# A chunked state-space scan inside a fused network: the order of SyncE's loads, and the place and buffers of the column sums of squares

## The chip, the cores and the metric

The kernel runs on one core of a Trainium2 chip. The metric is the device time of one execution in microseconds, lower is better.

## What is computed

The kernel computes a whole block of layers on a float32 input x of 2 x 1024 x 128: a small feed-forward layer, attention, the feed-forward layer again, a mixture of experts with 8 experts, a bidirectional Mamba-2 layer, and the mixture of experts again. The change touches the Mamba-2 layer only. For each direction it is, cut to what matters:

```python
z, xBC, dt = split(u @ Wi.T)
xBC = silu(conv4(xBC) + conv_b)
x, Bm, Cm = split(xBC)
dt = softplus(dt + dt_bias); A = -exp(A_log)
h = h * exp(dt_t * A) + (dt_t * x_t) B_t        # for each time step t, from h = 0
y = einsum(h, C_t) + D * x
y = y * silu(z)
y = y * rsqrt(mean(y * y) + 1e-5) * norm_w      # mean over the 256 channels
out = y @ Wo.T
x = x + 0.5 * (out_forward + out_backward)
```

## The kernel before, in words

The layer has four units: two batches times two directions (`UNITS`). A unit has 8 chunks of 128 time steps, so there are N = 32 chunks, g = 8u + i, where i is called the step below. The recurrence is done in chunks. Within a chunk a 128 x 128 matrix of decays per head takes the place of the time loop, and a state h is passed from chunk to chunk. All five engines run a program written out by hand, each a loop over g in its own order, and they meet only at semaphores; an engine that waits holds up all that is behind it in its program.

What happens for chunk g, with the lines of the profile:

- SyncE, `spread_rows` (L1917): one DMA spreads the four rows of running sums of the chunk over all 128 partitions into `cums[g % 2]` (L1922). It waits until ScalarE's Relus have read the place (`lowered`). If i > 0, two more DMAs bring the exponentials of these sums, the decays, into `e_cum[g % 2]` (L1929). They wait for `y_read` of g - 1, which is VectorE's read of the outputs of chunk g - 2. Ahead of chunk 16, `keep_rows` writes the sums of the second batch to DRAM and waits for the write.
- TensorE, `before` (L2053): transposes of x, the product of B and C, and a transpose of B (L2067) that raises `b_done`.
- ScalarE, `exps` (L2072): four Relus on `cums` (L2081), a copy of the transposed B to `mb_bs` (L2086, waits for `b_done`), one exponential (L2088).
- VectorE, `front`: `xdt` (L2106), `gm` (L2110), `mt` (L2113, waits for the exponential).
- GpSimd, `to_state` (L2125) and `decay` (L2144); TensorE, `state` (L2136); VectorE, `pass_state` (L2159).
- TensorE, `outputs` (L2168, L2172, L2178), all into one PSUM bank; VectorE, `back` (L2191, L2193), which raises `y_read`.
- The gate, y * silu(z) (L2202), on GpSimd in units 0 to 2 and on VectorE in unit 3; ScalarE squares the result into `y2[g % 2]` (L2211); GpSimd adds the two halves, `pair` (L2215); TensorE multiplies with a column of ones, `squares` (L2228), which gives the sum of squares of 128 time steps.
- Once per unit: `variance` on VectorE (L2235) and `deviation` on ScalarE (L2242, a square root, which needs its own activation table, as the exponential and the silu do).
- The output projection of unit u - 1 runs within unit u, in three parts: TensorE `output` (L2258), VectorE `add` (L2269 to L2276), at steps 3, 4 and 5. It shares a PSUM bank with the column sums, so `squares` waits for `out_read` of the parts that were added before.

Beside this, unit u prepares unit u + 1: TensorE projects (L2005) in pieces, ScalarE takes them (L2019) and makes the first tap of the convolution (L2032), VectorE makes the other three (L2041), two of them at each of the steps 0 to 5, and at step 6 ScalarE runs four silus over 1024 columns (L2048) and those of z. In unit 3 GpSimd scatters the rows of one routing for the next mixture of experts (L1555) between its other work, and the last scatter has to be done before the second mixture can load its first slots.

In loop g the engines work in this order. TensorE: `before(g+1)`, `state(g)`, projections, `outputs(g)`, `squares(g-2)`, `output`. ScalarE: `exps(g+1)`, `square(g-1)`, then `deviation`, takes and taps. VectorE: `front(g+1)`, `pass_state(g)`, `back(g)`, `add`, taps. GpSimd: `to_state(g+1)`, gate of g, `decay(g+1)`, `pair(g-1)`.

## Time and profile before

| | |
|---|---|
| runs | 864.51, 865.79, 862.6 us; median 864.51 |
| the profiled execution | 858.66 us, its span 856.9 us |
| TensorE matmuls busy | 717.7 us (84%) |
| ScalarE busy | 544.5 us (64%) |
| VectorE busy | 494.1 us (58%) |
| GpSimd busy | 300.5 us (35%) |
| stretch of the scan | about 491 to 695 us |

The busy shares are averages over stages that differ: in the attention stage ScalarE and TensorE are full, in the mixtures TensorE is, in the scan it is VectorE for most of the time. A share over the span says little about what a change in one stage is worth. The profiled execution lies below the three timed runs, so terms that are read from it are applied as a difference.

### The profile page before, as it was taken

Reading aid. Unit: us, or ns where it says so; the run is one execution under the profiler, and the core shown is the slowest. Engines: PE = TensorE matmul, PEld = TensorE weight load, DVE = VectorE, ACT = ScalarE, POOL = GpSimd, SP = SyncE. Lnnn points to the kernel's source line nnn. Section 1 sums busy time; section 2 is a strip of 40 time slices with the busy share of each in tenths; the row PEclk is TensorE's granted clock in tenths of the full one; section 3 lists DMA queues with packets and bytes.
Section 4 is the critical chain, followed back from the end, with each engine's and each line's share of the span. In section 5 each row is a group of like instructions: output and inputs, shape, how many; then the busy total and the mean of one; then the engine's idle time right before and its main releaser. Section 6 shows DMA issues by size and latency. Waiting matters only on the chain.

```text
span 856.9 us, 12889 instructions
## 1 busy us (share of the span) xinstructions
PE 717.7 (84%) x3968; PEld 372.2 (43%) x3968; DVE 494.1 (58%) x1450; ACT 544.5 (64%) x938; POOL 300.5 (35%) x331
## 2 busy tenths in 40 slices
PE   4799999989999879877889886888878868899981
PEld 1432222212232225544556454666556645556650
DVE  6876532215754747632656479787898857233341
ACT  5378997989989976523456775966967514234440
POOL 3090003301000515264123555444642832644343
PEclk9899999999999999997989988889998978899996
DMA  4057652521791202111211031212221311111313
GB/s 129 2 197 181 149 112 54 214 83 50 263 211 51 87 25 60 30 53 38 72 28 55 26 108 46 69 43 66 73 69 40 109 48 31 58 47 51 86 44 94
DMA packets 76361, 69.70 MB, mean 81 GB/s; under 512 B 9732, under 2 KB 60281, under 8 KB 76032
## 3 DMA queue, kind: packets, MB, share of 16 engines
q1 hardware_dynamic: 70880, 60.04, 25.0%
q0 software_dynamic: 5120, 8.68, 3.1%
q8 instruction: 35, 0.57, 0.3%
q14 instruction: 38, 0.31, 0.1%
q10 hardware_dynamic: 288, 0.10, 0.1%
HBM read 40.70 MB, written 29.18 MB: 82 GB/s over the span
## 4 chain that ended last, share of the span: by engine, by line
PE 27%; DVE 12%; issue 10%; ACT 7%; POOL 3%; DMA 2%; SPq 0%; POOLq 0%; DVEq 0%; ACTq 0%
PE ps_main L1628 11%; PE ps_main L1658 8%; DVE mb_act L2041 4%; PE ps_side L2005 1%; PE ps_main L1589 1%; PE ps_main L1624 1%; POOL moe_slots L1555 1%; ACT mb_act L2048 1%; DMA moe_back<-moe_rows 1%; PE ps_main L1699 1%; ACT mb_e_seg L2081 1%; DVE moe_hid L1653 1%; POOL moe_rows L1726 1%; DVE mb_h L2159 1%; DVE mb_xdt L2106 1%
## 5 line engine op out<-in xcount | busy, mean ns | idle before, releaser
L685 ACT ACTIVATE attn_p<-attn_ps 128x1024 f32<-128x1024 f32 x256 | 240.5, 1059 | 34.2 <-PE attn_ps L701 19.9
L1628 PE MATMUL ps_main<-moe_xsT,moe_w 128*128 128x320 f32 x384 | 131.8, 471 | 18.7 <-issue 9.9
L701 PE MATMUL attn_ps<-attn_p,attn_v 128*32 128x512 f32 x1024 | 136.6, 604 | 3.9 <-issue 3.7
L1638 ACT ACTIVATE moe_act_h<-ps_main 128x320 f32<-128x320 f32 (+1 forms) x128 | 55.2, 433 | 115.9 <-PE ps_main L1628 53.1
L1653 DVE TENSOR_TENSOR moe_hid<-moe_act_h,ps_main 128x320 f32<-128x320 f32 (+1 forms) x128 | 62.0, 485 | 113.3 <-ACT moe_act_h L1638 48.8
L1555 POOL DMA_INDIRECT moe_slots<-rows,moe_scatter_at x64 | 63.5, 991 | 98.1 <-issue 34.5
L678 PE MATMUL attn_ps<-attn_q_rows,attn_k_rows 64*128 64x512 bf16 x448 | 84.0, 385 | 12.2 <-ACT attn_p L685 5.3
L1628 PEld LDWEIGHTS ps_main<-moe_xsT,moe_w 128*128 128x128 f32 x384 | 70.3, 200 | 53.8 <-issue 34.4
L1658 PE MATMUL ps_main<-moe_hid,moe_w 128*128 128x320 f32 (+1 forms) x256 | 80.9, 493 | 7.9 <-issue 4.7
L678 PEld LDWEIGHTS attn_ps<-attn_q_rows,attn_k_rows 64*128 64x128 bf16 x448 | 20.4, 92 | 134.3 <-ACT attn_p L685 119.3
L1726 POOL DMA_INDIRECT moe_rows<-moe_y,moe_dest x48 | 46.1, 961 | 87.0 <-ACT moe_y L1719 63.3
L2041 DVE SCALAR_TENSOR_TENSOR mb_act<-mb_padded,mb_taps,mb_act 128x1024 f32<-128x1024 f32 x48 | 67.1, 1408 | 3.1 <-ACT mb_act L2032 2.6
L1658 PEld LDWEIGHTS ps_main<-moe_hid,moe_w 128*128 128x128 f32 (+1 forms) x256 | 45.1, 208 | 40.0 <-issue 22.7
L2081 ACT ACTIVATE mb_e_seg<-mb_cums,mb_cum_col 128x128 f32<-128x128 f32 x128 | 40.7, 389 | 28.6 <-DMA mb_cums<-mb_cum_kept 28.6
L1193 POOL TENSOR_TENSOR x_sb<-x_sb,bout_half 128x1024 f32<-128x1024 f32 (+1 forms) x4 | 7.3, 1830 | 103.7 <-DVE rows L1148 103.7
L2202 POOL TENSOR_TENSOR mb_z<-mb_y_in,mb_z 128x256 f32<-128x256 f32 x24 | 26.2, 1093 | 49.2 <-DVE mb_y_in L2193 37.1
L434 POOL TENSOR_SCALAR attn_parts<-attn_q 128x512 bf16<-128x512 f32 x4 | 2.5, 617 | 111.8 <-DVE attn_q L396 111.8
L701 PEld LDWEIGHTS attn_ps<-attn_p,attn_v 128*32 128x32 f32 x1024 | 20.5, 107 | 41.4 <-issue 36.2
L2113 DVE TENSOR_TENSOR mb_mt<-mb_e_seg,mb_gm 128x512 f32<-128x512 f32 x32 | 26.7, 836 | 17.6 <-ACT mb_e_seg L2088 9.9
L1726 POOL DMA_INDIRECT moe_rows<-mb_y,moe_dest x24 | 22.9, 955 | 34.9 <-ACT mb_y L1719 28.8
L2005 PE MATMUL ps_side<-norm_xT,mb_w_xbc 128*128 128x512 f32 x64 | 31.7, 616 | 3.2 <-DVE mb_ab L1974 1.9
L2136 PE MATMUL ps_main<-mb_xw,mb_bs 128*128 128x256 f32 x56 | 19.8, 438 | 15.5 <-DVE mb_h L2159 10.7
(268 smaller groups left out, 1283.5 us busy)
## 6 DMA issues: line engine op xcount, KB each, us to landing
mb_cums<-mb_cum_kept SPq DMA_DIRECT2D x32, 256.0 KB
moe_slots<-zeros SPq DMA_DIRECT2D x4, 1380.0 KB, 13.7
attn_q_rows<-attn_q_parts SPq DMA_DIRECT2D x36, 128.0 KB
attn_k_rows<-attn_k_parts SPq DMA_DIRECT2D x36, 128.0 KB
moe_w<-in_w SPq DMA_DIRECT2D x3, 1536.0 KB, 11.7
moe_rows<-zeros SPq DMA_DIRECT2D x4, 1024.0 KB, 15.1
moe_back<-moe_rows SPq DMA_DIRECT2D x16, 256.0 KB, 3.3
mb_e_cum<-mb_e_cum_kept SPq DMA_DIRECT2D x56, 64.0 KB
```

The lines of the kernel that those rows point to most:

```text
L678: ins = self.core.nc.tensor.matmul(into, self.k_rows[rows, ring, pair, keys], self.q_rows[rows, ring, pair, queries], start=True, stop=True)
L685: self.core.nc.scalar.activation(self.p[:, w % self.PB, :, :].rearrange("p a n -> p (a n)"), self.ps_s[:, w % self.SB, :, :].rearrange("p ...
L701: ins = self.core.nc.tensor.matmul(self.ps_av[32 * i:32 * i + 32, :], self.v[:, b * TPB + kt, HGROUPS * i + m, :], self.p[:, w % self.PB, ...
L1555: nc.gpsimd.indirect_dma_start(self.slots[r], bass.IndirectOffsetOnAxis(self.scatter_at[:, b, k, j:j + 1], 0), self.row_of[:, b * TPB + j, ...
L1628: self.core.nc.tensor.matmul(ps[:, w % 2, 0:CAP], wt[:, e, c * P:(c + 1) * P], self.xsT[:, u % 2, :], start=True, stop=True).then_inc(self ...
L1638: self.core.nc.scalar.activation(self.act_h[into, w % 2, :], self.ps_h1[rows, w % 2, 0:CAP], ACT.Silu).then_inc(self.silu_done, 1)
L1653: self.core.nc.vector.tensor_tensor(self.hid[rows, u % 2, c, :], self.act_h[rows, w % 2, :], bank[rows, w % 2, 0:CAP], ALU.mult)\
L1658: return self.core.nc.tensor.matmul(self.y_bank(u)[:, 0:CAP], self.w2[rows, u % E_, c, :], self.hid[rows, u % 2, c, :], start=start, stop= ...
L1726: self.core.nc.gpsimd.indirect_dma_start(self.rows[u // E_], bass.IndirectOffsetOnAxis(self.dest[0:n, u % self.OUT, s:s + 1], 0), self.y[u ...
L2005: self.core.nc.tensor.matmul(bank[:], weight, self.xT[:, t0:t0 + BANK], start=True, stop=True).then_inc(self.proj_done, 1)
L2041: ins = self.core.nc.vector.scalar_tensor_tensor(out, src, tap, out, ALU.mult, ALU.add)
L2081: ins = nc.scalar.activation(self.e_seg[:, g % 2, hh, :], self.cums[:, g % 2, hh, :], ACT.Relu, bias=self.cum[:, di, n, hh:hh + 1], scale= ...
```

## The change

Three things are changed, all in the scan.

1. SyncE's loads. `spread_rows` is split into `spread_sums` and `spread_decays`. Chunks 0 and 1 are as before. From there the order is sums(2), sums(3), decays(2), sums(4), decays(3), and so on: the sums of chunk g come ahead of the decays of chunk g - 1. The conditions that each waits for are unchanged.
2. The column sums of squares. `y2` has three places in place of two (1 KB more in each partition), ScalarE's `square` waits accordingly for the column sum of three chunks earlier, and TensorE runs `squares(g-3)` ahead of `outputs(g)` where it ran `squares(g-2)` behind it. In the last three loops it is as before (loop 29 has both).
3. The scale of a finished unit. VectorE's `variance` of unit u - 1 moves within step 2 from ahead of `front` to behind `back`; ScalarE's `deviation` moves from step 2 to step 3.

```diff
-        self.y_in, self.y_old, self.y2 = sb("y_in", [P, 2, 2, P]), sb("y_old", [P, 2, 2, P]), sb("y2", [P, 2, 2, P])
+        self.y_in, self.y_old, self.y2 = sb("y_in", [P, 2, 2, P]), sb("y_old", [P, 2, 2, P]), sb("y2", [P, 3, 2, P])
...
-    def spread_rows(self, sp, g):
+    def spread_sums(self, sp, g):
         u, di, b, i, n, cols = self.at(g)
         j = n % TPB
         if g >= 2:
             sp.wait_ge(self.lowered, g - 1)
         sp.dma_start(self.cums[:, g % 2, :, :], self.cum_dram[b, di, j].unsqueeze(0).to_broadcast([P, NH, P])).then_inc(self.cums_in[g % 2], 16)
+
+    def spread_decays(self, sp, g):
+        u, di, b, i, n, cols = self.at(g)
+        j = n % TPB
         if i == 0:
             return
         if g >= 2:
...
-        if g >= 2:
-            act.wait_ge(self.ss_done, g - 1)
-        self.core.nc.scalar.activation(self.y2[:, g % 2, :, :], self.z[:, u % 2, :, cols], ACT.Square).then_inc(self.squared, 1)
+        if g >= 3:
+            act.wait_ge(self.ss_done, g - 2)
+        self.core.nc.scalar.activation(self.y2[:, g % 3, :, :], self.z[:, u % 2, :, cols], ACT.Square).then_inc(self.squared, 1)
...
+                    parts = (0 if u == 0 else PARTS_OUT * (u - 1) + min(max(i - 3, 0), PARTS_OUT)) + (u == 3 and i == 7)
+                    if 3 <= g < N - 2:
+                        mamba.squares(pe, g - 3, parts)
                     mamba.outputs(pe, g)
-                    if g >= 2:
-                        mamba.squares(pe, g - 2, (0 if u == 0 else PARTS_OUT * (u - 1) + min(max(i - 3, 0), PARTS_OUT)) + (u == 3 and i == 7))
+                    if g >= N - 3:
+                        mamba.squares(pe, g - 2, parts)
...
                         for g in range(2):
-                            mamba.spread_rows(sp, g)
+                            mamba.spread_sums(sp, g)
+                            mamba.spread_decays(sp, g)
                         moe.fetch(sp, 1)
-                        for g in range(2, N):
+                        for g in range(2, N + 1):
                             if g == 2 * NC:
                                 mamba.keep_rows(sp, 1)
-                            mamba.spread_rows(sp, g)
+                            if g < N:
+                                mamba.spread_sums(sp, g)
+                            if g >= 3:
+                                mamba.spread_decays(sp, g - 1)
...
-                    if u >= 1 and i == 2:
-                        mamba.variance(dve, u - 1)
                     if u == 3 and i == 6:
                         mamba.variance(dve, 3)
...
                     mamba.back(dve, g)
+                    if u >= 1 and i == 2:
+                        mamba.variance(dve, u - 1)
...
-                    if u >= 1 and i == 2:
+                    if u >= 1 and i == 3:
                         mamba.deviation(act, u - 1)
```

## Rows read from the trace of the kernel before

**Rows 1.** Busy time over four stretches of the scan: this is their sum.

```profile
sum 204.00, PE 163.04 PEld 118.71 DVE 167.05 ACT 145.05 POOL 110.65; mean PE 40.76 PEld 29.68 DVE 41.76 ACT 36.26 POOL 27.66
```

**Rows 2.** Waits of ScalarE, 491 to 695 us: total, times, longest.

```profile
ACT mb_e_seg L2081 <- DMA mb_cums<-mb_cum_kept: 28.6, 15, 3.6
```

**Rows 3.** Waits of SyncE's queue, 491 to 695 us.

```profile
SPq L1929 <- DVE mb_y_in L2193: 119.9, 21, 12.9
```

**Rows 4.** Timeline of SyncE: start, duration, instruction.

```profile
622.79 1.24 SPq L1929 DMA_DIRECT2D mb_e_cum<-mb_e_cum_kept  x2
...
629.73 1.23 SPq L1929 DMA_DIRECT2D mb_e_cum<-mb_e_cum_kept  x2
631.00 0.59 SPq L1922 DMA_DIRECT2D mb_cums<-mb_cum_kept  x1
```

**Rows 5.** Timeline of ScalarE in unit 2; in brackets the idle time before.

```profile
613.65 1.28 ACT L2242 ACT_TABLE_LOAD   x1
...
634.51 1.28 ACT L2081 ACTIVATE mb_e_seg<-mb_cums,mb_cum_col 128x128 f32<-128x128 f32 x4 [3.56 <-DMA mb_cums<-mb_cum_kept]
```

**Rows 6.** Timeline of VectorE, units 1 to 3.

```profile
564.59 0.42 DVE L2191 TENSOR_TENSOR mb_y_old<-mb_e_cum,ps_main 128x256 f32<-128x256 f32 x1 [1.77 <-PE ps_main L2178]
...
576.64 0.87 DVE L2276 SCALAR_TENSOR_TENSOR x_sb<-ps_main,mb_rstd,x_sb 128x128 f32<-128x128 f32 x3
...
589.48 2.89 DVE L2041 SCALAR_TENSOR_TENSOR mb_act<-mb_padded,mb_taps,mb_act 128x1024 f32<-128x1024 f32 x2
...
600.86 0.69 DVE L2113 TENSOR_TENSOR mb_mt<-mb_e_seg,mb_gm 128x512 f32<-128x512 f32 x1 [3.12 <-ACT mb_e_seg L2088]
...
620.69 0.96 DVE L2113 TENSOR_TENSOR mb_mt<-mb_e_seg,mb_gm 128x512 f32<-128x512 f32 x1 [0.52 <-ACT mb_e_seg L2088]
...
646.00 0.18 DVE L1142 RECIPROCAL norm_rstd<-norm_std 128x4 f32<-128x4 f32 x1 [1.86 <-ACT norm_std L1113]
```

**Rows 7.** Timeline of GpSimd in unit 3.

```profile
664.36 0.61 POOL L2125 TENSOR_TENSOR mb_xw<-mb_xdt,mb_to_end 128x256 f32<-128x256 f32 x1 [2.04 <-DVE mb_xdt L2106]
...
692.53 0.99 POOL L1555 DMA_INDIRECT moe_slots<-rows,moe_scatter_at  x1 [0.16 <-issue]
```

**Rows 8.** Timeline of ScalarE at the turn from unit 1 to 2.

```profile
583.54 0.42 ACT L2211 ACTIVATE mb_y<-mb_z 128x256 f32<-128x256 f32 x1 [0.96 <-POOL mb_z L2202]
587.31 1.28 ACT L2081 ACTIVATE mb_e_seg<-mb_cums,mb_cum_col 128x128 f32<-128x128 f32 x4 [3.35 <-DMA mb_cums<-mb_cum_kept]
588.57 0.27 ACT L2086 COPY mb_bs<-ps_main 128x128 f32<-128x128 f32 x1
...
591.65 4.26 ACT L2048 ACTIVATE mb_act<-mb_act,mb_conv_b 128x1024 f32<-128x1024 f32 x4
...
596.67 0.60 ACT L2019 ACTIVATE mb_z<-ps_side 128x512 f32<-128x512 f32 x1 [0.28 <-PE ps_side L2005]
```

**Rows 9.** Timeline of TensorE's matmuls in unit 1.

```profile
576.56 1.06 PE L2168 MATMUL ps_main<-mb_act,moe_hid 128*128 128x128 f32 x4
...
586.60 0.38 PE L2228 MATMUL ps_main<-mb_ones,mb_y 128*128 128x1 f32 x2 [0.66 <-POOL mb_y L2215]
...
588.26 0.27 PE L2067 MATMUL ps_main<-ident,mb_act 128*128 128x128 f32 x1
...
592.73 0.48 PE L2228 MATMUL ps_main<-mb_ones,mb_y 128*128 128x1 f32 x2 [2.01 <-POOL mb_y L2215]
593.08 3.55 PE L2005 MATMUL ps_side<-norm_xT,mb_w_z 128*128 128x512 f32 x4
```

**Rows 10.** Timeline of TensorE's matmuls, other places.

```profile
564.47 0.59 PE L2228 MATMUL ps_main<-mb_ones,mb_y 128*128 128x1 f32 x2
...
629.57 1.88 PE L2005 MATMUL ps_side<-norm_xT,mb_w_z 128*128 128x512 f32 x4
...
633.59 0.38 PE L2228 MATMUL ps_main<-mb_ones,mb_y 128*128 128x1 f32 x2 [0.66 <-POOL mb_y L2215]
```

**Rows 11.** Busy time and granted clock (PEclk) of one stretch.

```profile
590.00:597.00 7.00, 4.99 (x21) 2.63 (x20) 4.64 (x8) 6.71 (x9) 3.40 (x3) 0.76 0.33 107
```

More of the change, by code:

```diff
@@ L2208, in square @@
         act.wait_ge(self.gate_done, g + 1)
-        if g >= 2:
-            act.wait_ge(self.ss_done, g - 1)
-        self.core.nc.scalar.activation(self.y2[:, g % 2, :, :], self.z[:, u % 2, :, cols], ACT.Square).then_inc(self.squared, 1)
+        if g >= 3:
+            act.wait_ge(self.ss_done, g - 2)
+        self.core.nc.scalar.activation(self.y2[:, g % 3, :, :], self.z[:, u % 2, :, cols], ACT.Square).then_inc(self.squared, 1)
     def pair(self, pool, g):
         pool.wait_ge(self.squared, g + 1)
-        self.core.nc.gpsimd.tensor_tensor(self.y2[:, g % 2, 0, :], self.y2[:, g % 2, 0, :], self.y2[:, g % 2, 1, :], ALU.add).then_inc(self.paired, 1)
+        self.core.nc.gpsimd.tensor_tensor(self.y2[:, g % 3, 0, :], self.y2[:, g % 3, 0, :], self.y2[:, g % 3, 1, :], ALU.add).then_inc(self.paired, 1)
     def squares(self, pe, g, parts):
@@ L2227, in squares @@
         col = 3 * D + n % TPB
-        self.core.nc.tensor.matmul(self.ps_o[:, col:col + 1], self.y2[:, g % 2, 0, :], self.ones[:, 0:1], start=True, stop=True).then_inc(self.ss_done, 1)
+        self.core.nc.tensor.matmul(self.ps_o[:, col:col + 1], self.y2[:, g % 3, 0, :], self.ones[:, 0:1], start=True, stop=True).then_inc(self.ss_done, 1)
     def variance(self, dve, k):
```

## The prediction

> **What bounds the kernel now.** I went from the stage totals to the waits of single engines and then to the timelines around those waits. The scan is the stretch from 491 to 695 us; nothing outside it is touched. In it VectorE is busy 167.05 of 204 us, ScalarE 145.05 and TensorE 163.04 [rows 1]. So VectorE is the engine whose idle time counts, 37 us of it. The change is aimed at another engine's wait: ScalarE stands 28.6 us in 15 places before the four Relus of a chunk (L2081), each time for the transfer of `mb_cums` [rows 2]. The queue that issues these transfers shows why: SyncE stands 119.9 us in 21 places at L1929, the issue of the decays, until VectorE has read the outputs of an earlier chunk [rows 3]. The sums of the next chunk are queued behind. One such place: decays at 629.73, sums only at 631.00 [rows 4], Relus at 634.51 after 3.56 us of idling [rows 5].
>
> The reader has to keep apart which of these waits reach VectorE. Over most of a unit VectorE works without a gap (convolution taps, `front`, `back`), and a ScalarE that waits 2 or 3 us there is late for nobody. The gaps of VectorE that matter here are few [rows 6]: 3.12 us at 600.86 before `mt` of chunk 16 (the turn from unit 1 to 2), 0.52 at 620.69, 1.86 at 646.00 (the turn from 2 to 3, waiting for ScalarE's root), 1.77 at 564.59 (waiting for TensorE's outputs). From 664.36 the last unit is set by GpSimd, which goes from one piece to the next until its sixteenth scatter at 692.53 [rows 7]; what is won before 664 is kept, what is won after it in ScalarE or VectorE is worth nothing.
>
> **SyncE's order.** `sums(g+1)` is now issued behind `decays(g-1)` and no longer behind `decays(g)`, so it waits for VectorE one chunk further back. Two neighbouring issues of decays are at 622.79 and 629.73, 6.9 us apart [rows 4]; from issue to the Relus it takes 631.00 to 634.51, 3.5 us [rows 4, 5]. Going up to 6.9 us earlier, the transfer has landed where ScalarE now stands 3.56 us. I take all of the 28.6 us of waiting as gone, the three places of the squares costing nothing by themselves. SyncE issues the same three transfers for a chunk. `decays(g)` stands behind one issue more, which waits for the Relus of chunk g-1; those are done before the outputs that `decays(g)` has to wait for anyway, so it stays on time. At the start `sums(3)` now shares the queues with the four loads of the combine; I price it at nothing (the decays behind it could be late by at most the 0.6 us of one issue).
>
> What does the vanished wait bring? At the turn from unit 1 to 2, ScalarE squares at 583.54 and then stands 3.35 us until 587.31 for the sums of chunk 15. The Relus could start at 583.96. But after them, in the same queue, comes the copy of the turned B (`mb_bs`), at 588.57 [rows 8], and it needs TensorE's `before(15)`, whose last matmul starts at 588.26 and lasts 0.27 [rows 9]. ScalarE works in order, so the exponential, the table loads and the silus of the next unit stay behind this copy. The wait for the DMA is replaced by a wait for TensorE, and what TensorE gives back is the gain.
>
> The Trainium skill (DMA: Bandwidth & Descriptors, Rules for kernel authors) says to issue a DMA early and wait on its semaphore late, so that its fixed cost overlaps. By that rule all 3.35 us would be gained at this turn; by the row of the copy almost none of it is. I go by the row and keep the rule's outcome as a rival.
>
> **Column sums one chunk later, ahead of the outputs.** Before, TensorE ran `squares(g-2)` behind `outputs(g)`, and stood there for GpSimd's pair: 0.66 us at 586.60, 2.01 us at 592.73 [rows 9], 0.66 us at 633.59 [rows 10]. With chunk g-3 the pair is long done and these waits go. At 586.60 and 633.59 the column sums stand right before the output matmuls and `before(15)`, `before(23)`: the copy on ScalarE comes 0.66 earlier at each turn. At the first turn it also ends a 0.28 us wait for the projection of z at 596.67 [rows 8], because this projection (593.08) no longer stands behind the 2.01 us. So the turns give -0.66-0.28 = -0.94 and -0.66.
>
> It has two prices. First, the two matmuls now lie before `outputs(g)`. Mostly TensorE waits there for VectorE's read of the last chunk and it is hidden; where TensorE is the late one, at 564.59, the whole of it shows: 0.59 us for the two [rows 6, 10], against 0.38 at 586.60, part of which lies under the next matmul's start. Bounds 0 and 0.59; I take +0.45, near the upper, since nothing else stands between there. Second, the column sums wait for `out_read`, the adds of the last output part, and that wait now holds `outputs(g)` as well at steps 4, 5 and 6 of a unit. At step 4 of unit 1 the adds end at 576.64+0.87 = 577.51 [rows 6], while the outputs started at 576.56 [rows 9]: 0.95 us later, plus the sums. Some of it is caught up before the turn (the pair's wait is gone, and the outputs, of which the first group took 1.06 at 576.56, may fall into a faster stretch). From below it costs 0, from above 0.95 plus the 0.59 of the slow pair, 1.5; it is nearer to the lower end, since TensorE stood idle for 0.66 in the next step. I take +0.4. The same step of unit 2 comes without the sums of the next batch ahead of it; I price it at nothing, with the same 0.95 as its upper bound.
>
> **Root one step later.** `variance` goes behind `back`, `deviation` from step 2 to step 3: the table loads, 1.28 us each [rows 5], are as many as before, in another place. At step 2 of unit 2 they made ScalarE late for `mt` by 0.52 [rows 6]; at step 3 VectorE has the three adds of an output part (0.87 at 576.64 [rows 6]) and their scale to do first, which covers it. -0.52. In units 1 and 3 both places are under other work.
>
> **Sum.** +0.45 +0.4 -0.94 -0.52 -0.66 = -1.27 us. The profiled execution took 858.66 us (span 856.9 and 1.76 around it), so its like would take 857.4. The median of the three runs before lies 5.85 above that execution, at 864.51; the difference of -1.3 applied to it gives 863.2 us. Half a per cent (4.3 us) is about what a measurement of this kernel can tell from no change; this is well inside.
>
> **The rivals.**
> *The wait is paid back in full.* If `before(15)` and `before(23)` come early enough, ScalarE is bound only by VectorE's last taps, which start at 589.48 and end at 592.37 [rows 6]. The last of the four silus (from 591.65, 4.26 for four [rows 8]) could start at 592.4 in place of 594.8: -2.4. At the next turn the whole 1.86 goes. -2.4-1.86-0.52+0.45 = -4.3: 860.2 us. For it: 28.6 us of measured waiting. Against it: TensorE's 588.26 one line before the copy.
> *Nothing changes.* The gaps just move: TensorE's outputs late by `out_read` eat the 0.94 and 0.66, the time stays at 864.5. For it: VectorE is full, and GpSimd sets the last 30 us.
> *TensorE's clock.* Idle time that is now in pieces (0.66, 2.01) gathers in one place in front of the outputs. After the 2.01 us wait the projection of z ran 3.55 us, against 1.88 at 629.57 [rows 9, 10]; the granted clock of this stretch is 0.76 on the mean [rows 11], so it had been at the lower of its two levels, 1.2 GHz, for about half of it. If step 4 of unit 1 waits 0.95 us longer (its outputs are slow already, 1.06 at 576.56), the projection behind it costs 1.67 more, and each of the three groups of the outputs about 0.5 (1.06 less 1.06*1.88/3.55), 1.5 together. All of it reaches VectorE: 864.5+0.45+0.95+1.67+1.5 = 869.1 us, so it is slower from the point where one projection and one set of outputs per scan go to the low clock, and a second such step in unit 2 would add 3.2 more. Against it: in the rows before, VectorE stands for TensorE's outputs in one place of this kind only, 564.59.
>
> **Chances.** Forecast 0.5, own range 861.5 to 864.5; full gain 0.17; nothing 0.2; the clock 0.13. The range for 8 in 10 reaches from below the full gain, 859.8, to 867.0, between nothing and the clock. Faster by over 0.5% (under 860.2): half of the full gain and a tail of the forecast whose costs fail to show, 0.17. Slower by over 0.5%: most of the clock's chance, 0.1. Within: 0.73.
>
> **What the profile after would show.** ScalarE's wait at L2081 for `mb_cums` falls from 28.6 to under 5 us, and in its place a wait at the copy L2086 for L2067 of TensorE appears, 2 to 3 us at the two turns. TensorE's wait for GpSimd at L2228 goes (right), or stays (the pair is not the releaser). TensorE's wait before the column sums for VectorE's adds (L2276) of about 1 us at step 4 shows the second price. The 0.52 before `mt` at step 2 of unit 2 is gone. The 3.12 at the turn is still above 2. The scan gets 1 to 2 us shorter. The prediction is wrong if the copy L2086 doesn't wait (full gain), if the granted clock in the scan falls in more stretches than before, or if the decays become a wait of VectorE at L2191.

## The result, and the profile after

The changed kernel took 859.28 us (median of 20 executions, 849.66 to 866.31), the kernel before beside it 863.16 us (median of 20). The ratio is 0.9935 with a 95% interval of 0.9912 to 0.9957: 3.9 us between the medians, 3.7 to 7.6 us by the interval. The forecast was 1.3 us off, 863.2, with a range down to 859.8. (The kernel before was itself 1.35 us under the 864.51 from which the forecast started.) The profiled execution took 854.94 us, span 853.1.

Single executions of one kernel spread over some 15 us here, and a ratio leaves out those more than 1.5% above the fastest, which cuts into that spread. So below, where kernels are compared, the difference is that of the means over all executions, with 1.96 standard errors.

The lines of the profile after that answer to those of before (all line numbers behind the edited `spread` functions are 4 higher). Busy time in the same four stretches of the scan [rows 1]:

```profile
sum 204.00, PE 159.15 PEld 118.85 DVE 166.71 ACT 145.74 POOL 112.59; mean PE 39.79 PEld 29.71 DVE 41.68 ACT 36.43 POOL 28.15
```

Waits of ScalarE, of SyncE's queue and of TensorE, 491 to 695 us (total, times, longest):

```profile
ACT mb_bs L2090 <- PE ps_main L2071: 20.6, 11, 4.1
```

```profile
SPq L1933 <- DVE mb_y_in L2197: 92.8, 22, 8.5
SPq L1922 <- ACT mb_e_seg L2085: 29.2, 8, 8.6
```

```profile
PE ps_main L2232 <- POOL mb_y L2219: 2.5, 3, 1.3
```

and the same wait of TensorE in the kernel before:

```profile
PE ps_main L2228 <- POOL mb_y L2215: 12.6, 12, 2.5
```

The 28.6 us that ScalarE stood for `mb_cums` [rows 2] are 1.3 in one place, as the line in the page's list of groups shows with its idle time at the end:

```profile
L2085 ACT ACTIVATE mb_e_seg<-mb_cums,mb_cum_col 128x128 f32<-128x128 f32 x128 | 40.5, 389 | 1.3 <-DMA mb_cums<-mb_cum_kept 1.3
```

In their place stand 20.6 us for TensorE's transpose of B (L2071), and the sums in SyncE's queue now wait for ScalarE's Relus of the chunk before. TensorE's wait for GpSimd's pair, 12.6 us in 12 places, is 2.5 in 3. Timelines of ScalarE at the two turns of a unit and of VectorE at the gaps of [rows 6]:

```profile
583.55 0.41 ACT L2215 ACTIVATE mb_y<-mb_z 128x256 f32<-128x256 f32 x1
583.85 1.26 ACT L2085 ACTIVATE mb_e_seg<-mb_cums,mb_cum_col 128x128 f32<-128x128 f32 x4
588.35 0.27 ACT L2090 COPY mb_bs<-ps_main 128x128 f32<-128x128 f32 x1 [3.23 <-PE ps_main L2071]
...
633.72 0.27 ACT L2090 COPY mb_bs<-ps_main 128x128 f32<-128x128 f32 x1 [2.70 <-PE ps_main L2071]
```

```profile
563.76 0.42 DVE L2195 TENSOR_TENSOR mb_y_old<-mb_e_cum,ps_main 128x256 f32<-128x256 f32 x1 [1.03 <-PE ps_main L2182]
...
600.25 0.69 DVE L2117 TENSOR_TENSOR mb_mt<-mb_e_seg,mb_gm 128x512 f32<-128x512 f32 x1 [3.19 <-ACT mb_e_seg L2092]
...
619.74 0.80 DVE L2117 TENSOR_TENSOR mb_mt<-mb_e_seg,mb_gm 128x512 f32<-128x512 f32 x1
...
644.04 0.18 DVE L1142 RECIPROCAL norm_rstd<-norm_std 128x4 f32<-128x4 f32 x1 [1.02 <-ACT norm_std L1113]
```

The Relus of chunk 15 start 3.46 us earlier than at [rows 8] (583.85 for 587.31), and the copy behind them 0.22 earlier (588.35 for 588.57): the exchange of one wait for another that the prediction had. (By then the whole scan of this profile is 0.43 us ahead; counted from VectorE's `xdt` of chunk 14, the Relus come 3.0 us earlier and the copy 0.2 us later.) The gap at the first turn is 3.19 (it was 3.12), the 0.52 at 620.69 is gone, the 1.86 at the second turn is 1.02.

To place differences I cut the scan at VectorE's `xdt` (one for each of the 32 chunks) and number the steps between them from 0, so that step k runs from the `xdt` of chunk k to that of chunk k + 1 (step 15 is the end of the first turn, step 23 that of the second); and I count the second mixture from its first transpose (L1589) to its last addition to x. Of the two first profiles the start differs by 0.5 us, the scan from first `xdt` to first transpose by 1.0 (206.2 and 205.2), the mixture by 2.2 (156.3 and 154.1). More than half of what one pair of profiles shows lies where nothing was changed. That made two theories. **A:** the change acts in the scan alone, the rest is scatter. **B:** the second mixture gets shorter too.

### The profile page after: what moved, and what is told of

Read it like the earlier page. It is cut to its first block, busy times and chain, and to the rows that moved or that the text cites. A ratio compares the mean times of both kernels' runs of the same rounds, so it can differ in the third digit from the quotient of the medians.

```text
span 853.1 us, 12889 instructions
## 1 busy us (share of the span) xinstructions
PE 709.3 (83%) x3968; PEld 368.3 (43%) x3968; DVE 494.3 (58%) x1450; ACT 544.1 (64%) x938; POOL 302.9 (36%) x331
## 3 DMA queue, kind: packets, MB, share of 16 engines
q1 hardware_dynamic: 70880, 60.04, 25.7%
## 4 chain that ended last, share of the span: by engine, by line
PE 26%; DVE 13%; issue 11%; POOL 6%; DMA 2%; ACT 2%; another core or an unknown queue 1%; POOLq 0%; SPq 0%; DVEq 0%; ACTq 0%
PE ps_main L1628 11%; PE ps_main L1658 7%; DVE mb_act L2045 4%; POOL moe_slots L1555 1%; PE ps_side L2009 1%; PE ps_main L1589 1%; POOL moe_rows L1726 1%; PE ps_main L1624 1%; DVE moe_hid L1653 1%; DMA moe_back<-moe_rows 1%; POOL mb_z L2206 1%; POOL mb_h_dec L2148 1%; PE ps_main L1699 1%; POOL mb_xw L2129 1%
## 5 line engine op out<-in xcount | busy, mean ns | idle before, releaser
L1628 PE MATMUL ps_main<-moe_xsT,moe_w 128*128 128x320 f32 x384 | 128.6, 462 | 23.4 <-DVE moe_hid L1653 15.1
L1628 PEld LDWEIGHTS ps_main<-moe_xsT,moe_w 128*128 128x128 f32 x384 | 68.5, 195 | 57.7 <-issue 37.0
L1658 PE MATMUL ps_main<-moe_hid,moe_w 128*128 128x320 f32 (+1 forms) x256 | 76.6, 471 | 7.6 <-DVE moe_hid L1653 7.6
L1658 PEld LDWEIGHTS ps_main<-moe_hid,moe_w 128*128 128x128 f32 (+1 forms) x256 | 42.7, 197 | 37.4 <-issue 13.8
L2117 DVE TENSOR_TENSOR mb_mt<-mb_e_seg,mb_gm 128x512 f32<-128x512 f32 x32 | 27.3, 853 | 15.6 <-ACT mb_e_seg L2092 9.2
L2140 PE MATMUL ps_main<-mb_xw,mb_bs 128*128 128x256 f32 x56 | 20.0, 442 | 19.0 <-DVE mb_h L2163 11.8
```

Source lines behind the costliest of these rows:

```text
L1628: self.core.nc.tensor.matmul(ps[:, w % 2, 0:CAP], wt[:, e, c * P:(c + 1) * P], self.xsT[:, u % 2, :], start=True, stop=True).then_inc(self ...
L1658: return self.core.nc.tensor.matmul(self.y_bank(u)[:, 0:CAP], self.w2[rows, u % E_, c, :], self.hid[rows, u % 2, c, :], start=start, stop= ...
```

## The experiments

**First session: both kernels again, and two parts alone.** `before_again` and `after_again` are the two kernels. `order_only` has SyncE's new order alone. `squares_only` has the three places and

```diff
+                    if 3 <= g < N - 2:
+                        mamba.squares(pe, g - 3, parts)
                     mamba.outputs(pe, g)
-                    if g >= 2:
-                        mamba.squares(pe, g - 2, (0 if u == 0 else PARTS_OUT * (u - 1) + min(max(i - 3, 0), PARTS_OUT)) + (u == 3 and i == 7))
+                    if g >= N - 3:
+                        mamba.squares(pe, g - 2, parts)
```

> The kernel before once more, to see how far two profiled executions of one kernel differ, stage by stage. In the first one the scan (first mb_xdt of the scan to the first transpose of the second mixture) took 206.2 us and the second mixture 159.4. Theory A (the change acts in the scan alone, by 1 to 1.5 us, and the rest of the 5.6 us between the medians is the scatter of stretches that it doesn't touch): the second mixture of this run differs from 159.4 by 1 us or more, either way. Theory B (the change shortens the second mixture too, by 2.3 us): this one stays at 159.4 within 0.5. Ratio 1.000 within its interval in both.

> The changed kernel once more. Scan 205.2 us and second mixture 157.1 in the first profile. Theory A: scan 205 within 0.5, mixture anywhere between 157 and 160, ratio 0.997 to 0.999. Theory B: mixture at 157.1 within 0.5 and ratio about 0.9935.

> Only SyncE's order is changed, the column sums and the root stay. Theory A: ScalarE's wait for mb_cums goes from 28.6 to under 3 us, and as TensorE still reaches the transposes of B at the same time, the copy of B waits in its place, 20 us or more; the scan gets 0 to 0.3 us shorter, ratio 0.999 to 1.000. Rival (the loads pay by themselves): scan 1 us or more shorter.

> Only the column sums: three places, one chunk later, ahead of the outputs. Theory A: TensorE's waits for GpSimd's pair go (28 us of both queues to under 5), but ScalarE still waits for mb_cums at the turns, so the 0.66 us per turn is not gained; VectorE's variance at step 2 now stands ahead of front and waits for a column sum that comes one loop later, several us three times: the scan is 2 to 6 us longer, ratio 1.002 to 1.007. Rival (it pays alone): scan 0.7 us or more shorter.

**Second session, another chip: the scan by itself, and two edits beyond the change.** `cut_before` and `cut_after` end behind the scan: the second mixture's loops of all engines are empty and its additions to x are left out.

```diff
-                for u in range(HALF, 2 * HALF):
+                for u in range(0):
```

`early_b` takes the transpose of B out of `before(g)`:

```diff
+                    if g + 2 < N and (g + 2) % NC:
+                        mamba.turn_b(pe, g + 2)
```

right behind `outputs(g)`; the first two chunks and the first of each unit keep it at `before`. `warm_after` adds a filler to the changed kernel, matmuls whose results nobody reads, 20 ahead of the last column sums, 3 between them and 19 ahead of the second mixture:

```diff
+                def keep_busy(n):
+                    for _ in range(n):
+                        nc.tensor.matmul(mamba.ps_b[:, 0:P], core.ident[:], core.ident[:], start=True, stop=True)
```

> The kernel before with everything behind the scan left out (the second mixture and its sums; x is stored once the last standard deviation is there), so that its time is that of the start and the scan alone. In the profile the last variance ends at 694.7; with the root and the store some 8 us more: 703 to 708 us, and a scatter of less than the 4.2 us (standard deviation) that 67 runs of the whole kernel show, if that scatter comes from the second mixture. Theory A (the change acts in the scan alone): this kernel is above cut_after by about what the whole kernels differ by, 3.4 us over 67 and 32 runs (interval 1.7 to 5.1). Theory B (part of the gain is made behind the scan): it is above cut_after by only the 1.6 to 2.3 us by which the profiles' scans differ up to the 28th xdt.

> The changed kernel cut in the same way (second mixture left out). Theory A: 3 to 4 us below cut_before. Theory B: 1.5 to 2.3 us below cut_before, and the rest of the 3.4 us is made in a second mixture whose program is the same in both kernels.

> The changed kernel with TensorE's transpose of B for chunk g + 2 taken out of the group of chunk g + 2 and put directly behind the outputs of chunk g, ahead of the output projection. If the wait that now ends ScalarE's idle time in the scan is its copy of B waiting for that transpose (20.6 us, 11 times, the longest 4.1), the copy goes to under 5 us of waiting, and the steps at the turns of a unit get shorter by 2 us (first turn) and 1 us (second): 3 us in the scan, 855 us for the whole kernel. Rival: the copy is early, but VectorE's own work (167 of 204 us busy) sets the pace of the scan, and the gain is under 1 us: 857 to 858.

> The changed kernel with matmuls of the identity by itself (128 columns each, results not used) in TensorE's idle time at the end of the scan: 20 ahead of the last sums, 3 between them, 19 ahead of the first transpose of the second mixture. Granted clock in the ten microseconds before that mixture was 0.72 and in its first ten 0.64 to 0.77 in six profiles, and the mixture lasted 153.4 to 162.8 us from its first transpose to its last addition. Theory B (the mixture's length goes by TensorE's clock in its first 75 us): granted clock 1.0 in its first ten microseconds, the group of its fourth expert's transposes 1 to 3 us earlier against the first transpose, and 1 to 3 us off the whole. Theory A: the clock there is of no weight, or the filler costs its own 0.15 us each where it delays the sums: 0 to plus 1 us.

**Third session: the filler in both kernels (20, 3 and 11 matmuls), the changed kernel again, order with root.** `order_root` is parts 1 and 3 of the change, with the lines of its diff.

> The kernel before with the filler at the end of the scan (matmuls of the identity, results not used: 20 ahead of the last sums, 3 between them, 11 ahead of the first transpose of the second mixture), which in the changed kernel held TensorE's granted clock at 1.0 from 688 us to 798 us, and with it the second mixture at 143.7 us from first transpose to last addition, where six profiles without it had 153.4 to 162.8 and one on the same chip 149.6. If that is the clock's doing: 3 to 5 us below the kernel before, and the mixture's length within 1 us of the changed kernel's with filler. Rival: the length of 143.7 us was the changed kernel's own (theory B: its layout in memory), and stays 150 or more here.

> The changed kernel with the same filler as the kernel before beside it: 20, 3 and 11 matmuls (8 fewer than in the run before, whose last 19 took 4.49 us and held the first transpose back by some 1.3 us). Theory A with the clock as the scatter: below the kernel before with filler by what the scans differ by, 1.3 to 2.3 us (the cut kernels: 1.3 of the means, 1.7 of the medians). Theory B: below it by 3 us or more. Against the longer filler: 1 us less.

> The changed kernel once more, beside the kernel before on one chip. The mean of 32 earlier runs was 3.4 us under that of 67 runs of the kernel before (1.7 to 5.1). Theory A: 1.3 to 2.3 us, the rest of the 3.4 was scatter of the mixture. Theory B: 3 to 4 us again.

> The kernel before with SyncE's new order and with the root of the norm one chunk later (variance behind VectorE's back of the third chunk, deviation in the fourth), but with two places for the squares and the column sums where they were. Time from the first to the 28th xdt: before 172.6 (and 174.1), SyncE's order alone 171.3, the whole change 171.0 and 170.2; of this the 0.85 at the turn from unit 2 to 3 (22nd to 25th xdt 21.80 before, 21.68 with the order alone, 21.94 with the column sums alone, 20.95 with the whole) came only with all of it. If the root makes that gain: 20.9 to 21.1 there, and the scan is as short as the changed kernel's, so that the column sums and their third place do nothing. If it takes the column sums too: 21.7 there, and 171.2 in all.

**Fourth and fifth session: the other pairs of parts, both kernels profiled on one chip, both edits beyond the change together.** `order_squares` is parts 1 and 2, `squares_root` parts 2 and 3; `warm_early` is `early_b` with the filler of `warm_short`.

> The changed kernel without the root moved: SyncE's new order, three places, the column sums one chunk further on. At the turn from unit 2 to 3 ScalarE waits 3.56 us for the rows of its exponentials in the kernel before, 3.28 with the column sums alone, 3.43 for TensorE's transpose of B with the order alone, and 2.70 with the whole change. If the two parts cover each other (either wait stands alone when the other is gone): 2.70 us and 20.95 from the 22nd to the 25th xdt here too, and the root is worth nothing there. If the root is needed: 21.6 or more.

> The changed kernel with both edits that went beyond it: TensorE's transpose of B for chunk g + 2 directly behind the outputs of chunk g, and the filler of 20, 3 and 11 matmuls at the end of the scan. From the profiles: the scan up to the 28th xdt 169.5 us instead of 169.7 to 171.0 of the changed kernel, the second mixture 143 to 145 us instead of 146 to 157: 1 to 3 us under the changed kernel beside it. If the filler only trades the clock for its own time: within 1 us of it.

> The changed kernel, beside the kernel before on one chip, for the difference of the whole and of the sections. Three sessions gave 3.7, 3.9 and 0.9 us less, each with about 2 us of uncertainty. If the scan makes it alone: 1.3 to 2.5 us less again, the scan's sections as in the three other profiles (20.95 us from the 22nd to the 25th xdt).

> The kernel before, profiled on the same chip as the changed kernel: 21.7 to 22.0 us from the 22nd to the 25th xdt, 15.1 to 15.6 from the 25th to the 28th, and a time equal to that of the kernel before that it is measured against. Should its second mixture be as long as the changed kernel's within a microsecond, the whole difference is the scan's.

> Once more SyncE's order and the column sums without the root. In the first profile of it the clock was at half from 619.5 to 622.7 us, under the output projection that stands ahead of the transpose for which ScalarE's copy of B waits. With the clock whole there: if order and column sums make the gain together, 6.24 us from the 24th to the 25th xdt and 2.70 us of waiting at the copy. If the root is needed: 6.9 and 3.2 or more.

> The column sums one chunk further on with three places, and the root one chunk later, with SyncE's old order. The rows of the exponentials come by the old order: if they are the other half of the lock, 6.9 to 7.3 us from the 24th to the 25th xdt as in the kernel before, with ScalarE's wait for them at 3.3 us or more. If the column sums and the root make the gain alone: 6.24. The whole: within 1 us of the kernel before or under it by less than 1.5.

**What was measured.** Each kernel had 12 executions (the first two 20, the cut ones 6). The difference is to the mean of the kernel before in the same session (20 to 47 executions; 863.0 and 862.0 us in the first pair and the first session, 842.3 to 842.6 on the chips of the later ones).

| kernel | median us | difference of means, us | scan, xdt 0 to 27 | mixture |
|---|---|---|---|---|
| before, first profile | 863.16 | | 172.6 | 156.3 |
| before_again | 861.44 | -0.8 ± 2.3 | 174.1 | 158.3 |
| before_third | 842.47 | 0.0 ± 1.6 | 173.0 | 150.1 |
| after, first profile | 859.28 | -3.7 ± 2.4 | 171.0 | 154.1 |
| after_again | 857.92 | -3.9 ± 2.1 | 170.2 | 156.6 |
| after_third | 839.55 | -0.9 ± 2.1 | 170.3 | 145.8 |
| after_fourth | 840.38 | -2.0 ± 1.3 | 170.2 | 149.5 |
| order_only | 865.58 | +3.2 ± 2.1 | 171.3 | 163.5 |
| squares_only | 862.91 | +0.7 ± 2.3 | 172.6 | 158.8 |
| order_root | 844.11 | +3.1 ± 1.9 | 174.8 | 149.1 |
| order_squares | 844.06 | +0.6 ± 1.8 | 173.2 | 149.9 |
| order_squares_again | 842.70 | -0.1 ± 2.1 | 173.2 | 149.3 |
| squares_root | 840.74 | -2.0 ± 2.0 | 171.7 | 147.7 |
| warm_before | 841.80 | -1.7 ± 2.1 | 171.8 | 143.1 |
| warm_after | 837.79 | -4.3 ± 1.8 | 169.7 | 144.4 |
| warm_short | 839.73 | -1.8 ± 2.2 | 170.8 | 145.2 |
| early_b | 840.31 | -2.2 ± 1.6 | 169.5 | 150.3 |
| warm_early | 837.90 | -4.3 ± 1.8 | 167.9 | 146.5 |
| cut_before | 694.71 | | 171.7 | |
| cut_after | 693.04 | | 170.9 | |

The four comparisons of the two kernels, each weighted by its variance, give -2.4 ± 0.9 us (their four ratios, weighted likewise, -2.6 ± 1.1). Two more pairs bear on it: `cut_after` is 1.3 ± 1.6 us below `cut_before` by the means (693.1 and 694.4), and `warm_short` is 0.1 ± 2.8 us below `warm_before`, which have the same filler. With these two the six comparisons give -2.0 ± 0.8. The scans up to the 28th `xdt` are 171.7 to 174.1 us in the five profiles of the kernel before (whole, cut or with filler; mean 172.6) and 169.7 to 171.0 in the seven of the changed one (mean 170.4): -2.2. Up to the first transpose of the mixture they are 207.1 and 204.8 us on the mean of the uncut ones: -2.3. The mixtures of the two kernels on one chip are 150.1 and 149.5, and with filler 143.1 against 144.4 and 145.2.

So theory A holds: the 2.2 us of the scan are the 2.0 to 2.4 of the whole. Theory B falls: with filler the changed kernel's mixture isn't shorter. The 3.7 and 3.9 of the first sessions and the 0.9 and 0.1 of a later one are what a mean of 12 to 20 executions with a standard deviation of 2 to 5 us gives around it.

Several expectations missed. `cut_after` missed the 3 to 4 us of theory A, because I had taken the first difference for the true one, and `cut_before` took 694.7 us for 703 to 708. `order_only` has a scan 1.4 us shorter than the mean of before, where 0 to 0.3 was expected (0.4 us shorter than the shortest of before). `squares_only` was to be 2 to 6 us longer in the scan and is as long as the mean of before. `early_b` was to gain 3 us, with under 5 us of waiting at the copy: the copy waits 11.8 us in 7 places. `warm_before` was to be 3 to 5 us below the kernel before, and is 1.7. `order_root` and `order_squares` have neither the short nor the expected scan.

**Which part makes what.** Steps of the scan that differ, in us, from the timelines of VectorE; the last column is TensorE's granted clock in step 15. Each combination of parts has one profile, where no other number is given.

| kernels | steps 9 to 11 | 15 | 20 | 23 | clock, 15 |
|---|---|---|---|---|---|
| before, 5 profiles | 24.5 to 26.5 | 4.75 to 5.24 | 7.36 to 7.46 | 6.99 to 7.33 | 0.64 or 0.65 in 4 |
| order | 24.5 | 4.37 | 7.37 | 6.98 | 1.00 |
| column sums | 25.1 | 4.50 | 7.40 | 6.91 | 1.00 |
| order, root | 25.6 | 4.82 | 8.64 | 6.97 | 0.65 |
| order, column sums, twice | 25.7, 25.6 | 4.57, 4.74 | 7.36 | 6.88, 7.20 | 1.00 |
| column sums, root | 25.3 | 4.33 | 6.80 | 7.27 | 0.99 |
| the change, 7 profiles | 24.6, once 25.7 | 3.64 to 4.57 | 6.78 to 6.80 | 6.24 or 6.25 | 1.00 |
| and B earlier, twice | 25.9, 24.5 | 3.19, 2.79 | 6.79 | 5.47, 5.46 | 1.00 |

*Step 20 is the root's* where the column sums are with it: 7.4 to 6.8. Order and root show 8.64 there, but the clock was at 0.50 just before, VectorE stood 1.68 us for TensorE's outputs, and the profile is that of its slowest execution (852.8 us, median 844.1). The root has a price one step before: step 19 is 5.49 or 5.50 us in every profile in which it is moved and 5.33 to 5.35 in every other.

*Step 23 needs all three.* Its length goes with the start of ScalarE's copy of B ahead of the silus. From the `xdt` of chunk 21 that is 8.7 to 9.0 us before, 8.6 with the order and with order and root, 8.9 to 9.0 with the column sums, with order and column sums, and with column sums and root, 7.9 in all seven profiles of the change, and 6.5 with B turned earlier. What ends ScalarE's idle time ahead of the silus of the next unit is, by its timelines in `before_third`, `order_only`, `squares_root` and `after_fourth`:

```profile
624.41 1.28 ACT L2081 ACTIVATE mb_e_seg<-mb_cums,mb_cum_col 128x128 f32<-128x128 f32 x4 [3.46 <-DMA mb_cums<-mb_cum_kept]
```

```profile
634.21 0.27 ACT L2090 COPY mb_bs<-ps_main 128x128 f32<-128x128 f32 x1 [3.43 <-PE ps_main L2071]
```

```profile
621.39 1.28 ACT L2081 ACTIVATE mb_e_seg<-mb_cums,mb_cum_col 128x128 f32<-128x128 f32 x4 [3.73 <-DMA mb_cums<-mb_cum_kept]
```

```profile
626.37 0.27 ACT L2090 COPY mb_bs<-ps_main 128x128 f32<-128x128 f32 x1 [2.70 <-PE ps_main L2071]
```

Two conditions end within a few tenths of each other: the rows by DMA and B by TensorE. With the order alone the second takes over the wait of the first; with column sums and root alone the first stays. Neither moves step 23 out of the range of before by more than 0.1 us.

Order and column sums without the root should then have made it, and twice did not. TensorE's timeline and the granted clock of `order_squares_again` (windows of 1 us) show why:

```profile
617.55 0.35 PE L2232 MATMUL ps_main<-mb_ones,mb_y 128*128 128x1 f32 x2 [1.80 <-POOL mb_y L2219]
...
619.43 2.93 PE L2262 MATMUL ps_main<-mb_wo,mb_z 128*128 128x128 f32 x12
```

```profile
618.00:619.00 1.00, 1.00 (x11) 0.88 (x12) 0.96 (x2) 1.00 (x5) 0.00 (x0) 1.00 0.55 182
...
620.00:621.00 1.00, 1.00 (x7) 1.00 (x6) 0.90 (x3) 0.00 (x0) 0.61 (x1) 0.50 0.03 12
621.00:622.00 1.00, 1.00 (x7) 1.00 (x6) 1.00 (x3) 0.00 (x0) 0.00 (x0) 0.50 0.00 0
```

The clock is at the lower level from 619.4 to 622.8, after TensorE had stood 1.80 us for GpSimd's pair and worked for 1.8, and the output projection takes 2.93 us. The transpose of B for which the copy waits stands behind it. In `after_fourth` TensorE stands only 1.31 us in the same place: VectorE no longer waits 0.47 us for `mt` (the root's table load is gone from there), and the sum of its outputs, the gate and the pair that follow from it come 0.56 us earlier. The projection takes 1.60:

```profile
616.19 0.35 PE L2232 MATMUL ps_main<-mb_ones,mb_y 128*128 128x1 f32 x2 [1.31 <-POOL mb_y L2219]
...
618.06 1.60 PE L2262 MATMUL ps_main<-mb_wo,mb_z 128*128 128x128 f32 x12
```

That the half clock delays B is in these rows; that the longer idle time makes the clock fall is not shown: the three profiles with 1.80 or 1.83 us here have it (`squares_only` is the third, with a projection of 2.72) and the ten with 1.31 to 1.36 don't (the seven of the changed kernel, column sums with root, and the two with B earlier), but no run varied the idle time by itself.

*The root pays a debt of the column sums.* Put one chunk later while `variance` stays ahead of `front`, they make VectorE stand 1.53 us in step 10 of `squares_only` and 1.33 in both profiles of order and column sums; in the changed kernel `variance` comes behind `back` and doesn't wait in this place:

```profile
562.59 0.17 DVE L2235 TENSOR_SCALAR mb_var<-ps_main 128x8 f32<-128x8 f32 x1 [1.53 <-PE ps_main L2228]
```

**Beyond the change.** With B turned earlier, ScalarE's copy at the second turn waits 1.32 us in place of 2.70, and step 23 goes from 6.24 to 5.47 and 5.46. At the first turn the wait is 2.79 in `early_b` and 1.32 in `warm_early`, and step 15 goes to 3.19 and 2.79. Both timed comparisons are too wide for 0.8 to 2 us. With the filler the clock is at 1.00 in all of the first five stretches of ten microseconds of the mixture in `warm_after` and `warm_before`; in `warm_short` the third is at 0.83, in `warm_early` the first and the third. Without it the first is at 0.62 to 0.78 in all 14 profiles of whole kernels. The first ten microseconds of the mixture and the stretch around 740, first in the changed kernel, then in `warm_after`:

```profile
696.00:706.00 10.00, 9.40 (x42) 6.90 (x43) 6.21 (x25) 2.33 (x5) 0.00 (x0) 0.77 0.12 30
...
736.00:746.00 10.00, 5.20 (x17) 2.79 (x16) 1.95 (x4) 1.30 (x3) 5.74 (x7) 0.77 0.18 50
```

```profile
688.20:698.20 10.00, 9.42 (x55) 7.35 (x54) 7.89 (x31) 3.66 (x7) 0.00 (x0) 1.00 0.10 23
...
728.20:738.20 10.00, 10.00 (x41) 6.59 (x40) 3.13 (x9) 4.71 (x14) 7.56 (x9) 1.00 0.22 65
```

Four mixtures with filler lasted 143.1 to 146.5 us, the eight without it in the later sessions 145.8 to 150.3. The filler isn't free. SyncE's first load of the mixture (L1572) is issued 3.5 to 3.6 us after the start of GpSimd's last scatter in the four profiles with filler and 2.3 to 2.5 in all 14 without, and the first transpose waits for this load. In `after_fourth` and in `warm_short`:

```profile
683.04 0.99 POOL L1555 DMA_INDIRECT moe_slots<-rows,moe_scatter_at  x1 [0.17 <-issue]
...
685.38 0.38 SPq L1572 DMA_DIRECT2D moe_xs<-moe_slots  x1
```

```profile
680.23 0.99 POOL L1555 DMA_INDIRECT moe_slots<-rows,moe_scatter_at  x1 [0.17 <-issue]
...
683.73 0.38 SPq L1572 DMA_DIRECT2D moe_xs<-moe_slots  x1
```

So the mixture starts some 1.3 us later, with 11 matmuls in the last group as with 19: the 1.3 us that the expectation of `warm_short` puts down to the last eight are not theirs. Why the load comes later is open. `warm_early`, with both edits, is at 837.9 us, 4.3 ± 1.8 below the kernel before and 2.3 ± 2.0 below the changed kernel of its session.

## Why the prediction was wrong

The direction was right, and so were the three gains: forecast -2.12 us together, measured -2.08. The steps that failed are the two costs of the column sums: +0.45 and +0.4 were forecast, -0.5 and 0 were measured. So the size was too small by 0.9 to 1.1 us. The rest of the miss is not the change's: the kernel before was 1.35 us under the time from which the forecast started, and the first comparison of the two showed 1.3 to 1.5 us more than all comparisons together support. Without these two pieces of chance the time would have been in the range. By the prediction's steps:

- **The wait for `mb_cums` is replaced, not paid back**: right. 28.6 became 1.3, and the copy L2090 waits 3.23 and 2.70 at the turns, close to the forecast ("2 to 3"). The rival "paid back in full" asked for a second turn shorter by 1.86; step 23 is 0.9 shorter on the mean, and with the order alone (6.98) as long as the shortest of before (6.99). The rule of the Trainium skill (DMA: Bandwidth & Descriptors, Rules for kernel authors) to issue early and wait late does what it says to the wait; what that is worth here is decided by the next thing the engine waits for.
- **Root, -0.52**: step 20 is 0.6 shorter and step 19 0.16 longer, -0.44. Right. That it was also needed to keep `variance` from standing 1.5 us was not in the working.
- **Second turn, -0.66**: step 23 is 0.75 to 1.1 shorter, -0.88 on the mean. Right in size, and in that the column sums are needed; I hadn't seen that they give nothing without the other two parts.
- **First turn, -0.94**: steps 12 to 15 are 24.4 us on the mean of five before and 23.6 after: -0.76. Right on the mean, in other portions: the copy comes 0.35 us earlier (15.9 and 15.5 us from the `xdt` of chunk 12), not 0.66. In four of five profiles of before the clock in step 15 is at 0.64 or 0.65 after TensorE's 2.01 us wait for the pair [rows 9], and TensorE reaches the transposes of chunk 16 up to 0.6 us after the last silu; in all seven after, that wait is gone, the clock is 1.00 there, and the transposes follow within 0.1 us. The half clock is not all of it, though: in `before_third`, with 1.00, step 15 is the longest of the five (5.23), because its sums arrived late and the silus with them. The rival about TensorE's clock expected more half clock here and there is less. That the wait makes the clock fall is not shown: with order and root it is 2.01 us and the clock 0.65, with the order alone 2.01 us and 1.00.
- **The price of two matmuls ahead of `outputs(g)`, +0.45**: failed. I had read 0.59 us from a stretch at half clock. With the clock whole the outputs in step 11 start 0.14 us behind the first of the two, and VectorE's wait for them is 0.73 us in `warm_before` and `cut_before` and 1.02 or 1.03 in six of seven profiles of the changed kernel: +0.3. But steps 9 and 10 are 0.25 us shorter, so that at a whole clock steps 9 to 11 go from 24.45 to 24.56. And the kernel before had that whole clock in only two of five profiles; in the others the wait was 1.36, 1.77 [rows 6] and 2.75, after the change it was 2.03 once. On the mean steps 9 to 11 are 0.5 us shorter, not 0.45 longer. Whether the change makes the half clock rarer here is open: `squares_root` waited 1.72 and `early_b` 2.19 us in this place. Nor is it the only place of its kind, as the working had it: at 499.12 VectorE stands 1.87 us for TensorE's outputs too (L2195), and 1.84 to 2.87 after the change.
- **The price of `out_read`, +0.4**: failed. The outputs of step 4 of unit 1 start later (577.31 for 576.56 [rows 9]; from the `xdt` of their chunk 5.07 us for 3.56, the full 1.5 of the upper bound), and yet steps 12 to 14 are as long as before (6.94, 6.22 or 6.55, 6.13). VectorE has its taps to do and doesn't notice; in other profiles of before these outputs start up to 5.7 us after `xdt` as well. The wait for the adds is seen at step 6, and it reaches nobody either. Measured: 0.

```profile
589.16 0.35 PE L2232 MATMUL ps_main<-mb_ones,mb_y 128*128 128x1 f32 x2 [0.42 <-DVE x_sb L2280]
```

- **Not in the sum**: steps 24 to 26 are 14.9 to 15.1 us after and 15.1 to 15.6 before, -0.35; steps 0 to 8 are 56.8 on the mean after and 56.3 before, +0.43, with ranges that overlap; steps 16 to 18 are 0.27 longer. Which part of the change makes these, if any does, is not settled.

The sum with the measured terms, means of seven profiles less means of five: +0.43 (steps 0 to 8), -0.47 (9 to 11), -0.76 (12 to 15), +0.27 (16 to 18), -0.44 (19 and 20), -0.88 (21 to 23), -0.35 (24 to 26), together -2.20.

What stays open: why SyncE's order alone was 3.2 ± 2.1 us slower as a whole when its scan was 1.4 us shorter. Its one profile has the longest mixture of all, 163.5 us, with a granted clock of 0.64 and 0.54 in its first and third ten microseconds; but `after_again`, on the same chip, has 0.66 and 0.53 there and a mixture of 156.6, so these two stretches don't explain it. Order and root, 3.1 ± 1.9 us slower, has an ordinary mixture (149.1), and one profile of its slowest execution doesn't say where the time goes. Whether the filler alone makes the kernel faster is not settled by any one comparison: 1 to 2 us in three, each with 2 to 3 us of uncertainty.

## What to carry to other kernels

Before costing a wait that goes, look at what else the same engine waits for right behind it: two conditions that end within some tenths of a microsecond lock each other, and a change that loosens one measures as nothing until the other is loosened too. Ask of a delay on an engine off the path whether anyone notices it: the outputs here came 1.5 us later and no step got longer. Read the granted clock beside each duration that becomes a price: the same output projection took 2.93 us at half clock and 1.60 at the whole. Where single executions scatter by 4 us, a few hundred nanoseconds are found in steps between landmarks of several profiles, not in times.

## What the runs showed of the hardware

- TensorE's granted clock fell in the same place of the program in all three profiles in which TensorE had stood idle for 1.80 or 1.83 us there (0.50 from 619.4 to 622.8 us in one, 1.8 us of work after the idling) and in none of the ten with 1.31 to 1.36 us. The output projection took 2.93 us in the one and 1.60 in the changed kernel.
- Matmuls of the identity in TensorE's idle time went with a granted clock of 1.00 through the first 50 us of the work behind them in two profiles, and of 0.83 in one or two stretches of ten microseconds in two others; in all 14 profiles of whole kernels without them the first such stretch was at 0.62 to 0.78. SyncE's next load was issued 1.1 us later behind the scatter ahead of it in all four, for a reason that no run shows.
- The kernel before took 862 to 863 us in the first two sessions and 842 to 843 on the chips of the later ones. Its scan was as long on all of them (171.7 to 174.1 us); the start was 6 to 17 us shorter on the later ones and the mixture 6 to 8 us.
